# Expert tiles of 256 gathered rows instead of 512 in the mixture-of-experts stage, with three weight buffers

## The chip, the cores and the metric

One NeuronCore of one Trainium2 chip runs the whole program. The metric is the device time of one execution in microseconds (us). The kernel before takes 4466.64 us, the median of three runs (4465.85 to 4473.64).

## The reference

Four layers follow each other on x of shape (4, 1024, 256): L0 to L3, each an attention against a context of 77 tokens and then a block of its own (L0: causal self-attention and a mixture of experts; L1: a ternary MLP; L2: a butterfly MLP; L3: a self-attention with selected heads). The change concerns the mixture of experts of L0:

```
logits = flat @ gate_W + gate_b                    # 4096 tokens x 8 experts
top_v, top_i = top_k(logits, 2); w = softmax(top_v)
for e in range(8):
    mid = gelu(flat @ exp_W1[e] + exp_b1[e])       # 256 -> 1024
    out += w_full[:, e:e+1] * (mid @ exp_W2[e] + exp_b2[e])   # 1024 -> 256
```

Only the two chosen experts of a token have a weight that isn't zero, so 8192 pairs of token and expert are worth computing.

## The kernel before, in words

The program has three phases, parted by barriers. Phase 0 runs the two attentions and the gate of L0 for each of the 4 batches. It writes the normalised tokens to DRAM (`d_xn`), the tokens themselves to `d_s`, and for each pair of token and expert an entry (token, gate weight) to the table `d_tab`, which has a region of 4096 places for each expert. It also splits the expert weights into a high and a low f16 half and stores them in `d_moe`, 2 MB for an expert (two DMAs of 1024 KB). Phase 1 is the expert stage. Phase 2 runs all the rest, batch by batch.

**The expert stage** works on tiles of TILE = 512 gathered rows of one expert. The number of tiles is a constant: NTILE (line 33) is the most that 8192 entries on 8 experts can need, 23 for 512 rows. All are run, whatever the gate chose; tiles without entries work on rows that nobody reads. At its start VectorE works out the expert and the region of each tile (lines 2290 to 2307), one column for each tile. Then each tile i goes through these steps, and every engine has its order written out by hand:

- SyncE (SP), lines 695 to 735: `tile_table(i)` waits until the stores of tile i-4 have landed, reads the tile's numbers into registers and loads 512 table entries (line 703). `tile_weights(i)` waits for the last matmul of tile i-2, loads the 2 MB of weights into `Wm[i % 2]` (line 712), and the bias columns into `b1t[i % 2]` (line 716). SP runs two tiles ahead. In its iteration 2 it also loads the context keys and values for phase 2 (`load_keys`, lines 556 to 559).
- GpSimd (POOL), lines 1719 to 1743: `pick_rows(i)` gathers the rows in TC4 = 4 indirect DMAs of 128 rows (line 1725); `add_rows(i - 2)` follows it and adds the results to `d_s` in 4 indirect DMAs (line 1734), after VectorE has written them and the adds of the tile before have landed.
- TensorE (PE): `turn_rows(i)` transposes the picked rows in 8 transposes (line 1226), in the middle of tile i-1, after `up(i-1, 4)`. `up(i, m)`, m = 0 to 7, computes 128 hidden channels for the 512 rows by `split3` (lines 806 to 808: high by high, high by low, low by high), 6 matmuls of 512 columns. `down(i, m)` adds the part of hidden group m to the output, 12 matmuls of 256 columns, one triple for each 128 rows, with 2 bias matmuls more for each 128 rows at m = 7 (lines 1252, 1253). `down` runs two steps behind `up`.
- ScalarE (ACT): `rows_affine(i)` (line 1594, two instructions) takes the transposed rows with scale and shift; line 1607 is the Gelu of each `up`.
- VectorE (DVE): `rows_parts` and the eight `halves` of a tile split values into f16 halves (lines 1912 and 1914); `rows_out(i - 1)` (line 2321, one instruction for each 128 rows) multiplies the output of the tile before by the gate weights, after `halves` of m = 3.

The order of PE's work:

```
for n in range(len(order) + 2):
    if n < len(order):
        up(*order[n])
        if order[n][1] == 4 and order[n][0] + 1 < NTILE:
            turn_rows(order[n][0] + 1)
    if n >= 2:
        down(*order[n - 2])
```

and POOL's:

```
for i in range(NTILE + 2):
    if i < NTILE:
        pick_rows(i)
    ...
    if i >= 2:
        add_rows(i - 2)
```

Of the kernel before, what the change touches and what calls it, by code (L numbers as in the profile page):

```python
# [7 lines left out]
P = 128  # L8
NB, T, D, TC = 4, 1024, 256, 77
NT = T // P  # L10
KD = D // P
# [192 lines left out]
def build(nc, A, out, known, stages):  # L204
    led = Ledger(known)
    with ExitStack() as ctx:
# [63 lines left out]
        def area(kb, n, dt=F32, rows=P):  # L270
# [35 lines left out]
        before_p, idf, tile_n, row_n = route[:, 0:P], route[:, 128:136], route[:, 136:136 + NTILE], route[:, 160:161]  # L306
# [13 lines left out]
        over = route[:, 816:816 + NTILE * NE].rearrange("p (i e) -> p i e", e=NE)  # L320
        passed = route[:, 1000:1000 + NTILE * NE].rearrange("p (i e) -> p i e", e=NE)
        tile_e, tile_j = route[:, 1184:1184 + NTILE], route[:, 1208:1208 + NTILE]
# [5 lines left out]
        sel = area(62.5, 32, F16)  # L328
# [3 lines left out]
        XTm = XT[:, :, :, :].rearrange("p s k c -> p (s k c)").rearrange("p (n s k c) -> p n s k c", n=2, s=2, k=KD)  # L332
# [74 lines left out]
        d_moe = dram("scr_expert_weights", [NE, 2, P, 2 * KD * HID], F16)  # L407


        names = ["pe", "act", "dve", "pool", "ld_next", "ld_kvw", "ld_const", "ld_kx", "st_kx0", "st_kx1", "st_vx0", "st_vx1", "st_mask", "ld_b12", "st_q0", "st_q1", "st_k0", "st_k1",  # L410
                 "ld_stack0", "ld_stack1", "ld_m0", "ld_m1", "ld_wexp0", "ld_wexp1", "st_wexp0", "st_wexp1",
                 "st_xn", "st_s", "st_tab", "ld_tab0", "ld_tab1", "ld_tab2", "ld_tab3", "ld_b10", "ld_b11", "ld_pick0", "ld_pick1",
                 "st_y", "ld_sel", "st_out"] + [f"{n}{g}" for n in ("ld_s", "ld_r") for g in range(NG)] + [
                 f"{n}{p}{c}" for n in ("st_qc", "ld_qc", "ld_mc") for p in range(2) for c in range(2)]
        sems = {n: ctx.enter_context(nc.semaphore("s_" + n)) for n in names}
# [77 lines left out]
        def _(sp):  # L493

            sp.dma_start(identf[:], A["c_ident"]).then_inc(once["low_w"], 16)
            sp.dma_start(d_tab, A["c_none"]).then_inc(once["kvw"], 16)
            sp.dma_start(route[:, 0:161], A["c_route"]).then_inc(once["kvw"], 16)
# [208 lines left out]
            def tile_weights(i):  # L706

                e = where[i][1]
                if i >= 2:
                    sp.wait_ge(*of("pe", "D", i - 2, NM - 1))  # L710
                for w in range(2):
                    sp.dma_start(Wm[i % 2][:, w].rearrange("p s n -> p (s n)"),
                                 d_moe[bass.ds(e, 1), w].rearrange("o p n -> p (o n)")).then_inc(*did(f"ld_wexp{i % 2}", i, w))
                if i >= 2:
                    sp.wait_ge(*of("act", "free", "U", i - 2, NM - 1))
                sp.dma_start(b1t[i % 2], A["exp_b1"][bass.ds(e, 1)].rearrange("o p m -> p (o m)")).then_inc(*did(f"ld_b1{i % 2}", i))
# [5 lines left out]
            sp.dma_start(b1b, A["L1_b1"].partition_broadcast(P)).then_inc(*did("ld_b12", 0))  # L722
            sp.dma_start(b2b, A["L1_b2"].partition_broadcast(P)).then_inc(*did("ld_b12", 1))
# [58 lines left out]
        def _(pe):  # L782
# [436 lines left out]
            def experts():  # L1219

                def turn_rows(i):
                    s = claim("A", "T", i)
                    pe.wait_ge(*of(f"ld_pick{i % 2}", i, TC4 - 1))
                    for c in range(TC4):
                        for k in range(KD):
                            mm = pe.transpose(s[:, k * TILE + c * P:k * TILE + (c + 1) * P], picked[:, i % 2, c, k * P:(k + 1) * P], identf[:])
                    mm.then_inc(*did("pe", "T", i))

                def up(i, m):
                    if m == 0:  # L1230
                        pe.wait_ge(*of(f"ld_wexp{i % 2}", i, 1))
                        pe.wait_ge(*of("dve", "xlo", i))
                    s = claim("A", "U", i, m)
                    w1 = Wm[i % 2][:, 0].rearrange("p s (k n) -> p s k n", k=KD)
                    for k in range(KD):
                        mm = split3(s[:, 0:TILE], parts(w1, k, slice(m * P, (m + 1) * P)), parts(XTm[:, i % 2], k), k == 0, k == KD - 1)
                    mm.then_inc(*did("pe", "U", i, m))

                def down(i, m):
                    n = i * NM + m  # L1240
                    if m == 0:
                        pair = ("B0", "B1") if i % 2 == 0 else ("S0", "S1")
                        acc[:] = [claim(pair[0], "D", i, 0), claim(pair[1], "D", i, 1)]
                    pe.wait_ge(*of("dve", "midlo", i, m))
                    w2 = Wm[i % 2][:, 1].rearrange("p s (m n) -> p s m n", m=NM)
# [10 lines left out]
                acc = [None, None]  # L1256
# [101 lines left out]
        def _(act):  # L1358
# [228 lines left out]
            def experts():  # L1587
# [11 lines left out]
                for i in range(NTILE):  # L1599
                    for m in range(NM):  # L1600
                        act.wait_ge(*of("pe", "U", i, m))
                        if m == 0:
                            act.wait_ge(*of(f"ld_b1{i % 2}", i))
# [3 lines left out]
                        act.activation(midf[:, n % 3], slot("U", i, m)[:, 0:TILE], ACT.Gelu, bias=b1t[i % 2][:, m:m + 1],  # L1607
                                       scale=1.0 / WS).then_inc(*frees("act", "U", i, m))
                        if m == 4 and i + 1 < NTILE:
                            rows_affine(i + 1)  # L1610
# [841 lines left out]
def layouts(i):  # L2452
# [37 lines left out]
    qs[0] = BIG  # L2490
    ks = z((MROW + 2 - 48, 2, GH, T), np.float16)
    ks[MROW - 48:] = 1.0
    route = z((P, 161), np.float32)
# [3 lines left out]
    route[:, 160] = np.arange(P) - BROW.index("e0")  # L2497
# [52 lines left out]
```

## Time and profile before

| what | value |
|---|---|
| median of three runs | 4466.64 us |
| the profiled execution's own time | 4502.6 us |
| its span | 4500.8 us |
| expert stage, first table step on DVE to the first load of phase 2 | 1641.3 to 2200.9 us of the span |
| PE / DVE / ACT / POOL busy over the whole span | 78% / 51% / 33% / 9% |
| HBM read and written over the span | 167.5 MB, 77.3 MB |

The profile is of one execution. Busy time of PE is a union of overlapping matmuls: successive matmuls start closer together than one of them lasts, so the distance of two starts, and not the duration, is what a matmul costs. A row of the groups has the line, the engine, the operation, out<-in by name, the shapes and the count; behind the bar stand the busy time in us and the mean duration in ns, then the idle time just before and what ended it.

### The profile page before, as it was taken

The page shows a single profiled execution, that of the slowest core. Times are in us where ns is not written, and L with a number is a line of the kernel's source. Part 1 is how long each engine was busy: PE and PEld are TensorE (multiplying, and loading weights), DVE is VectorE, ACT ScalarE, POOL GpSimd, SP SyncE. Part 2 cuts the span into 40 slices and gives each one's busy share as a digit, 9 for nine tenths or more (in the row PEclk, how much of TensorE's full clock was granted, in tenths as well). Part 3 has the DMA queues.
Part 4 walks back from the last instruction along what each step waited for, and adds up shares of the span by engine and source line. Part 5 has one row for each costly group of instructions (what it writes and reads, how often), then busy time and mean ns, then how long its engine had stood idle before and what let it go on. Part 6 is the DMA issues. An engine that isn't in the chain of part 4 may idle for free.

```text
span 4500.8 us, 51861 instructions
## 1 busy us (share of the span) xinstructions
PE 3497.8 (78%) x20322; PEld 1826.0 (41%) x20322; DVE 2298.6 (51%) x4977; ACT 1488.1 (33%) x2106; POOL 390.4 (9%) x298
## 2 busy tenths in 40 slices
PE   5278677667767749999778888788787896878969
PEld 2133332332332336666434433345343452444524
DVE  8765465565465335555463443643436534355343
ACT  2124333433334323333243322443224432234322
POOL 6000001001000124444200000000000000000000
PEclk7668868967877869999889989999899998999989
DMA  3221221231131056555401222012211113011130
GB/s 121 85 56 16 100 57 16 69 88 16 36 121 16 19 121 140 141 141 141 88 10 25 30 54 48 11 25 28 57 32 26 25 25 60 25 34 25 25 60 10
DMA packets 203902, 249.63 MB, mean 55 GB/s; under 512 B 99985, under 2 KB 166179, under 8 KB 191781
## 3 DMA queue, kind: packets, MB, share of 16 engines
q1 hardware_dynamic: 183945, 222.06, 19.3%
q0 software_dynamic: 19712, 24.20, 3.4%
q8 instruction: 167, 2.74, 0.3%
q14 instruction: 78, 0.63, 0.0%
HBM read 167.53 MB, written 77.25 MB: 54 GB/s over the span
## 4 chain that ended last, share of the span: by engine, by line
PE 53%; DVE 25%; ACT 7%; DMA 7%; issue 5%; SPq 2%; POOL 1%; another core or an unknown queue 1%; DVEq 0%; ACTq 0%; POOLq 0%
PE ps L806 5%; PE ps L808 5%; PE ps L807 5%; PE ps L1342 5%; DVE max_parts L1992 4%; PE ps L859 4%; PE ps L991 3%; PE ps L953 3%; PE ps L1199 2%; PE ps L1206 2%; PE ps L974 2%; ACT arena L1512 2%; PE ps L1127 2%; DVE minus_max_context L2136 2%; DMA q_stack<-scr_q 1%
## 5 line engine op out<-in xcount | busy, mean ns | idle before, releaser
L859 PE MATMUL ps<-ternary_W,ident 128*128 128x512 f16 x1552 | 496.2, 410 | 80.5 <-issue 25.4
L1992 DVE TENSOR_REDUCE max_parts<-ps 128x1 f32<-128x512 f32 (+3 forms) x768 | 388.5, 551 | 251.4 <-PE ps L956 151.8
L1444 ACT ACTIVATE arena<-ps 128x256 f32<-128x256 f32 (+7 forms) x512 | 321.4, 650 | 508.3 <-PE ps L974 289.2
L953 PE MATMUL ps<-k_stack,q_stack 96*128 96x512 f16 (+3 forms) x768 | 272.5, 390 | 101.0 <-DVE max_parts L1992 57.6
L1912 DVE CAST arena<-arena 128x512 f16<-128x512 f32 (+2 forms) x296 | 143.0, 483 | 316.1 <-ACT arena L1607 201.0
L974 PE MATMUL ps<-q_stack,k_stack 98*128 98x512 f16 (+3 forms) x768 | 257.6, 382 | 39.8 <-ACT arena L1444 24.4
L1512 ACT ACTIVATE arena<-ps 77x1024 f32<-77x1024 f32 x192 | 190.4, 1016 | 279.3 <-PE ps L1119 274.4
L859 PEld LDWEIGHTS ps<-ternary_W,ident 128*128 128x128 f16 x1552 | 153.4, 104 | 314.8 <-issue 113.7
L2414 DVE TENSOR_REDUCE max_parts<-ps 128x1 f32<-128x512 f32 x256 | 170.1, 688 | 176.1 <-PE ps L1317 174.1
L1342 PE MATMUL ps<-arena 128*96 128x512 f32 x512 | 246.1, 592 | 1.7 <-ACT arena L1671 1.7
L1914 DVE TENSOR_TENSOR arena<-arena 128x512 f16<-128x512 f32 (+2 forms) x296 | 239.0, 808 | 10.2
L1607 ACT ACTIVATE arena<-ps,arena 128x512 f32<-128x512 f32 x184 | 126.4, 687 | 354.9 <-PE ps L808 353.0
L1671 ACT ACTIVATE arena<-ps 128x1024 f32<-128x1024 f32 x128 | 130.5, 1023 | 338.6 <-PE ps L1331 338.6
L953 PEld LDWEIGHTS ps<-k_stack,q_stack 96*128 96x128 f16 x768 | 76.8, 103 | 339.1 <-DVE max_parts L1992 254.8
L806 PE MATMUL ps<-x_channels_hi_lo,arena 128*128 128x512 f16 x432 | 168.3, 389 | 52.4 <-DVE arena L2401 48.7
L808 PE MATMUL ps<-arena 128*128 128x256 f16 (+1 forms) x752 | 204.5, 272 | 0.0
L807 PE MATMUL ps<-arena 128*128 128x256 f16 (+1 forms) x752 | 204.4, 272 | 0.0
L806 PE MATMUL ps<-arena 128*128 128x256 f16 (+1 forms) x752 | 204.1, 272 | 0.0
L2136 DVE TENSOR_REDUCE minus_max_context<-ps 128x4 f32<-128x308 f32 x384 | 157.5, 467 | 86.6 <-PE ps L1103 85.4
L991 PE MATMUL ps<-arena 128*32 128x512 f32 (+3 forms) x1536 | 179.9, 552 | 13.5 <-ACT arena L1444 13.5
L1708 POOL DMA_INDIRECT scr_taken<-v_context,slots_of_batch x64 | 61.8, 966 | 1430.7 <-DVE slots_of_batch L2281 1412.4
L1734 POOL DMA_INDIRECT scr_x<-q_stack,arena x92 | 151.3, 1645 | 257.4 <-DVE q_stack L2321 236.4
(429 smaller groups left out, 7059.8 us busy)
## 6 DMA issues: line engine op xcount, KB each, us to landing
arena<-scr_expert_weights SPq DMA_DIRECT2D x46, 1024.0 KB
q_stack<-in_exp_W SPq DMA_DIRECT2D x16, 1024.0 KB
scr_expert_weights<-k_stack SPq DMA_DIRECT2D x16, 1024.0 KB, 4.9
q_stack<-scr_q SPq DMA_DIRECT2D x120, 128.0 KB, 3.8
scr_q<-arena SPq DMA_DIRECT2D x48, 256.0 KB, 2.9
k_stack<-scr_q SPq DMA_DIRECT2D x72, 128.0 KB, 4.1
scr_q<-arena SPq DMA_DIRECT2D x16, 512.0 KB, 4.3
scr_k<-arena SPq DMA_DIRECT2D x16, 512.0 KB, 4.5
```

The costliest lines, as they stand in the source:

```text
L806: pe.matmul(o, left[0], right[0], start=first, stop=False, **kw)
L807: pe.matmul(o, left[0], right[1], start=False, stop=False, **kw)
L808: return pe.matmul(o, left[1], right[0], start=False, stop=last, **kw)
L859: pe.matmul(s[:, 0:CH], ident[:], Wq1[:, 0, 0:CH], start=True, stop=True)
L953: mm = pe.matmul(s[:, 0:n], QS[0:MROW, buf, j, t * P:(t + 1) * P], KS[0:MROW, buf, j, c * CH:c * CH + n], start=True, stop=not on_edge)
L974: mm = pe.matmul(o, KS[0:MROW + 2, buf, j, kt * P:(kt + 1) * P], QS[0:MROW + 2, buf, j, a:(c + 1) * CH], start=True, stop=not edge)
L991: mm = pe.matmul(acc[c][QUARTER * j:QUARTER * (j + 1), a - c * CH:CH], v, p, start=kt == 0, stop=final, tile_position=(0, QUARTER * j))
L1342: pe.matmul(acc[c][0:TV], VP4[:, kt, h, :], PR4[:, (h * NT + kt) % NP, c * CH:(c + 1) * CH], start=kt == 0, stop=kt == NT - 1).then_inc(*d ...
L1444: act.activation(PR[:, n % NP, kt * P:T], slot(L, "ST", g, kt, j)[:, kt * P:T], ACT.Exp).then_inc(*did("act", L, "exp", g, kt, j))
L1512: act.activation(PRc[c][:, n % 3].rearrange("p i c -> p (i c)"), slot(L, "ST", c, g, jp)[0:TC], ACT.Exp).then_inc(*did("act", L, "exp", c, ...
L1992: dve.tensor_reduce(mpart[:, j * NT + t, c:c + 1], slot(L, "S", g, t, j, c)[:, 0:n], AX, ALU.max).then_inc(*frees("dve", L, "S", g, t, j, c))
L2136: dve.tensor_reduce(mine, slot(L, "S", c, g, t)[:, 0:GH * TC].rearrange("p (j c) -> p j c", c=TC), AX, ALU.max, negate=True).then_inc(*fre ...
```

## The change

TILE goes from 512 to 256, so NTILE goes from 23 to 39 and TC4 from 4 to 2. The three weight buffers `Wm[i % 3]` are the two of before and the space of the key stack `KS`, which phase 1 doesn't use otherwise. SP runs three tiles ahead; the bias columns have four buffers. Output accumulators of a tile are one PSUM bank (B0 or S0 by turns) where they were two. The tables of the start of the stage, which have 39 columns now, lie in the space of `XT`. The core of the diff:

```diff
-TILE = CH
+TILE = 2 * P
...
-        Wm = [area(16 + 16 * i, 2 * 2 * KD * HID, F16).rearrange("p (w s n) -> p w s n", w=2, s=2) for i in range(2)]
-        midf = area(48, 3 * CH).rearrange("p (n c) -> p n c", n=3)
-        mid = area(54, 4 * 2 * CH, F16).rearrange("p (n s c) -> p n s c", n=4, s=2)
+        Wm = [w.rearrange("p (w s n) -> p w s n", w=2, s=2) for w in (area(16, 2 * 2 * KD * HID, F16), area(32, 2 * 2 * KD * HID, F16),
+                                                                      KS[:, :, :, :].rearrange("p b h c -> p (b h c)"))]
+        midf = area(48, 3 * TILE).rearrange("p (n c) -> p n c", n=3)
+        mid = area(54, 4 * 2 * TILE, F16).rearrange("p (n s c) -> p n s c", n=4, s=2)
...
-        b1t = [area(63.25 + 0.0625 * i, NM) for i in range(2)]
+        b1t = [area(63.25 + 0.0625 * i, NM) for i in range(4)]
...
             def tile_weights(i):
                 e = where[i][1]
-                if i >= 2:
-                    sp.wait_ge(*of("pe", "D", i - 2, NM - 1))
+                if i >= 3:
+                    sp.wait_ge(*of("pe", "D", i - 3, NM - 1))
                 for w in range(2):
-                    sp.dma_start(Wm[i % 2][:, w].rearrange("p s n -> p (s n)"),
+                    sp.dma_start(Wm[i % 3][:, w].rearrange("p s n -> p (s n)"),
...
-                if i >= 2:
-                    sp.wait_ge(*of("act", "free", "U", i - 2, NM - 1))
+                if i >= 4:
+                    sp.wait_ge(*of("act", "free", "U", i - 4, NM - 1))
-                sp.dma_start(b1t[i % 2], ...)
+                sp.dma_start(b1t[i % 4], ...)
-            for i in range(2):
+            for i in range(3):
                 tile_table(i)
                 tile_weights(i)
...
             for i in range(NTILE):
-                if i + 2 < NTILE:
-                    tile_table(i + 2)
-                    tile_weights(i + 2)
+                if i + 3 < NTILE:
+                    tile_table(i + 3)
+                    tile_weights(i + 3)
...
-                        pair = ("B0", "B1") if i % 2 == 0 else ("S0", "S1")
-                        acc[:] = [claim(pair[0], "D", i, 0), claim(pair[1], "D", i, 1)]
+                        acc[:] = [claim("S0" if i % 2 else "B0", "D", i, 0)]
```

`tile_table`, `pick_rows`, `add_rows` and the orders of PE, ACT and DVE are the same in their text; their loops over TC4 have two passes instead of four.

## Rows read from the trace of the kernel before

**Rows 1.** The page: busy time, share of the span and instructions of each engine.
```profile
PE 3497.8 (78%) x20322; PEld 1826.0 (41%) x20322; DVE 2298.6 (51%) x4977; ACT 1488.1 (33%) x2106; POOL 390.4 (9%) x298
```

**Rows 2.** Busy time by stretch: us, busy us (count) by engine, granted clock, DMA share, GB/s.
```profile
1660.00:1700.00 40.00, 35.68 (x226) 23.49 (x227) 17.95 (x31) 12.62 (x18) 6.90 (x8) 0.88 0.45 144
1700.00:1800.00 100.00, 97.21 (x692) 67.89 (x691) 53.05 (x96) 31.08 (x45) 47.68 (x35) 1.00 0.67 136
```

**Rows 3.** Timeline of PE in a tile: start us, us, engine, line, operation.
```profile
1850.70 0.38 PE L806 MATMUL ps<-x_channels_hi_lo,arena 128*128 128x512 f16 x1
...
1852.00 0.27 PE L806 MATMUL ps<-arena 128*128 128x256 f16 x1
1852.11 0.27 PE L807 MATMUL ps<-arena 128*128 128x256 f16 x1
```

**Rows 4.** Chain that ended last, 1770 to 2195: start us, us, what (first, last of 17).
```profile
1793.09 0.87 PE ps L1226 x8
...
2154.47 0.87 PE ps L1226 x8
```

**Rows 5.** Groups by line and shape, expert stage.
```profile
L1914 DVE TENSOR_TENSOR arena<-arena 128x512 f16<-128x512 f32 x184 | 127.4, 693 | 6.3
L1607 ACT ACTIVATE arena<-ps,arena 128x512 f32<-128x512 f32 x184 | 126.4, 687 | 354.9 <-PE ps L808 353.0 <-DVE x_channels_hi_lo L1912 1.9
```

**Rows 6.** Groups by line and shape, whole span, ACT: one function at two widths.
```profile
L1444 ACT ACTIVATE arena<-ps 128x512 f32<-128x512 f32 x64 | 37.8, 597 | 74.4 <-PE ps L976 73.3
...
L1444 ACT ACTIVATE arena<-ps 128x256 f32<-128x256 f32 x64 | 23.0, 382 | 36.7 <-PE ps L976 36.6
```

**Rows 7.** Groups by line and shape, whole span, DVE: instructions of 256 columns.
```profile
L2200 DVE TENSOR_TENSOR x_tokens<-x_tokens,weights_flat 128x256 f32<-128x256 f32 x32 | 13.6, 425 | 1.1
...
L2082 DVE TENSOR_SCALAR arena<-arena 128x256 f16<-128x256 f32 x32 | 7.1, 283 | 0.0
```

**Rows 8.** Timeline of POOL: first add and last gather of one round.
```profile
1862.07 1.62 POOL L1734 DMA_INDIRECT scr_x<-q_stack,arena  x1 [9.72 <-DVE q_stack L2321]
...
1873.91 1.03 POOL L1725 DMA_INDIRECT x_tokens<-scr_x_normalised,arena  x1 [0.30 <-issue]
```

**Rows 9.** Busy time by stretch, after that last gather (columns as rows 2).
```profile
1877.00:1878.00 1.00, 1.00 (x6) 0.47 (x5) 0.00 (x0) 0.00 (x0) 0.00 (x0) 1.00 0.00 0
```

**Rows 10.** Chain in the one round beside the key loads: gather to landing.
```profile
1763.20 6.97 DMA x_tokens<-scr_x_normalised,arena
```

**Rows 11.** Timeline of SP's queue: weights, then the next table load.
```profile
1854.52 0.85 SPq L712 DMA_DIRECT2D arena<-scr_expert_weights  x2
...
1857.20 0.39 SPq L703 DMA_DIRECT2D arena<-scr_taken  x1
```

**Rows 12.** Timelines of SP's queue and POOL: table load behind the key loads, its reader.
```profile
1749.83 4.96 SPq L703 DMA_DIRECT2D arena<-scr_taken  x1
...
1759.20 1.01 POOL L1725 DMA_INDIRECT x_tokens<-scr_x_normalised,arena  x1 [5.52 <-DMA arena<-scr_taken]
```

**Rows 13.** DMA queues, 1855 to 1877: packets, MB, share of 16 engines.
```profile
q0 software_dynamic: 768, 1.05, 30.5%
q1 hardware_dynamic: 960, 2.11, 26.5%
```

**Rows 14.** Who waited for whom, 1665 to 2187: us, times, longest us.
```profile
PE ps L1226 <- DMA x_tokens<-scr_x_normalised,arena: 2.8, 1, 2.8
```

**Rows 15.** Timeline at the start of the stage: first transposes, first matmul of tile 0.
```profile
1660.63 1.97 PE L1226 MATMUL ps<-identf,x_tokens 128*128 128x128 f32 x8 [28.04 <-DMA x_tokens<-scr_x_normalised,arena]
...
1666.29 0.59 PE L806 MATMUL ps<-x_channels_hi_lo,arena 128*128 128x512 f16 x1 [3.69 <-DVE x_channels_hi_lo L1914]
```

**Rows 16.** Timeline at the end of the stage: last results on DVE, last add, next load.
```profile
2189.72 1.66 DVE L2321 TENSOR_SCALAR q_stack<-ps,arena 128x256 f32<-128x256 f32 x4 [2.86 <-PE ps L1253]
...
2197.22 1.55 POOL L1734 DMA_INDIRECT scr_x<-q_stack,arena  x1 [0.30 <-issue]
2200.94 0.39 SPq L521 DMA_DIRECT2D h_tokens<-scr_x  x1
```

More of the change, by code:

```diff
@@ L319, in build @@
         n_tiles, up_to = route[:, 800:808], route[:, 808:816]
-        over = route[:, 816:816 + NTILE * NE].rearrange("p (i e) -> p i e", e=NE)
-        passed = route[:, 1000:1000 + NTILE * NE].rearrange("p (i e) -> p i e", e=NE)
-        tile_e, tile_j = route[:, 1184:1184 + NTILE], route[:, 1208:1208 + NTILE]
-        Wm = [area(16 + 16 * i, 2 * 2 * KD * HID, F16).rearrange("p (w s n) -> p w s n", w=2, s=2) for i in range(2)]
-        midf = area(48, 3 * CH).rearrange("p (n c) -> p n c", n=3)
-        mid = area(54, 4 * 2 * CH, F16).rearrange("p (n s c) -> p n s c", n=4, s=2)
+        tables = XT[:, :, :, :].rearrange("p s k c -> p (s k c)").bitcast(F32)
+        over, passed = (tables[:, 320 * i:320 * i + NTILE * NE].rearrange("p (i e) -> p i e", e=NE) for i in range(2))
+        tile_e, tile_j = tables[:, 640:640 + NTILE], tables[:, 704:704 + NTILE]
+        Wm = [w.rearrange("p (w s n) -> p w s n", w=2, s=2) for w in (area(16, 2 * 2 * KD * HID, F16), area(32, 2 * 2 * KD * HID, F16),
+                                                                      KS[:, :, :, :].rearrange("p b h c -> p (b h c)"))]
+        midf = area(48, 3 * TILE).rearrange("p (n c) -> p n c", n=3)
+        mid = area(54, 4 * 2 * TILE, F16).rearrange("p (n s c) -> p n s c", n=4, s=2)
         tile_ids = area(62, 2 * NTILE).bitcast(I32)
-        sel = area(62.5, 32, F16)
+        sel = area(62.5, 64, F16)
         taken = [area(63 + 0.0625 * i, 2 * TC4).rearrange("p (c w) -> p c w", w=2) for i in range(4)]
-        b1t = [area(63.25 + 0.0625 * i, NM) for i in range(2)]
+        b1t = [area(63.25 + 0.0625 * i, NM) for i in range(4)]
         picked = X[:, :, :].rearrange("p (n c) d -> p n c d", n=2)
-        XTm = XT[:, :, :, :].rearrange("p s k c -> p (s k c)").rearrange("p (n s k c) -> p n s k c", n=2, s=2, k=KD)
+        XTm = XT[:, :, :, :].rearrange("p s k c -> p (s k c)")[:, 0:2 * 2 * KD * TILE].rearrange("p (n s k c) -> p n s k c", n=2, s=2, k=KD)
         q_f32 = QS[:, :, :, :].rearrange("p b h c -> p (b h c)").bitcast(F32)
@@ L496, in _ @@
             sp.dma_start(d_tab, A["c_none"]).then_inc(once["kvw"], 16)
-            sp.dma_start(route[:, 0:161], A["c_route"]).then_inc(once["kvw"], 16)
+            sp.dma_start(route[:, 0:200], A["c_route"]).then_inc(once["kvw"], 16)
             sp.dma_start(low_w, A["low_w"]).then_inc(once["low_w"], 16)
@@ L708, in tile_weights @@
                 e = where[i][1]
-                if i >= 2:
-                    sp.wait_ge(*of("pe", "D", i - 2, NM - 1))
+                if i >= 3:
+                    sp.wait_ge(*of("pe", "D", i - 3, NM - 1))
                 for w in range(2):
-                    sp.dma_start(Wm[i % 2][:, w].rearrange("p s n -> p (s n)"),
-                                 d_moe[bass.ds(e, 1), w].rearrange("o p n -> p (o n)")).then_inc(*did(f"ld_wexp{i % 2}", i, w))
-                if i >= 2:
-                    sp.wait_ge(*of("act", "free", "U", i - 2, NM - 1))
-                sp.dma_start(b1t[i % 2], A["exp_b1"][bass.ds(e, 1)].rearrange("o p m -> p (o m)")).then_inc(*did(f"ld_b1{i % 2}", i))
-            for i in range(2):
+                    sp.dma_start(Wm[i % 3][:, w].rearrange("p s n -> p (s n)"),
+                                 d_moe[bass.ds(e, 1), w].rearrange("o p n -> p (o n)")).then_inc(*did(f"ld_wexp{i % 3}", i, w))
+                if i >= 4:
+                    sp.wait_ge(*of("act", "free", "U", i - 4, NM - 1))
+                sp.dma_start(b1t[i % 4], A["exp_b1"][bass.ds(e, 1)].rearrange("o p m -> p (o m)")).then_inc(*did(f"ld_b1{i % 4}", i))
+            for i in range(3):
                 tile_table(i)
@@ L721, in _ @@
             sp.dma_start(KX[:MROW + 2], A["c_kx"]).then_inc(*did("ld_const", 0))
-            sp.dma_start(b1b, A["L1_b1"].partition_broadcast(P)).then_inc(*did("ld_b12", 0))
-            sp.dma_start(b2b, A["L1_b2"].partition_broadcast(P)).then_inc(*did("ld_b12", 1))
+            sp.dma_start(b1b, A["L1_b1"].partition_broadcast(P)).then_inc(*did("ld_rows12", 0))
+            sp.dma_start(b2b, A["L1_b2"].partition_broadcast(P)).then_inc(*did("ld_rows12", 1))
             for i in range(NTILE):
-                if i + 2 < NTILE:
-                    tile_table(i + 2)
-                    tile_weights(i + 2)
+                if i + 3 < NTILE:
+                    tile_table(i + 3)
+                    tile_weights(i + 3)
                 if i == 2:
@@ L1230, in up @@
                     if m == 0:
[L1231 removed]
+                        pe.wait_ge(*of(f"ld_wexp{i % 3}", i, 1))
                         pe.wait_ge(*of("dve", "xlo", i))
                     s = claim("A", "U", i, m)
[L1234 removed]
+                    w1 = Wm[i % 3][:, 0].rearrange("p s (k n) -> p s k n", k=KD)
                     for k in range(KD):
@@ L1254, in down @@
                     mm.then_inc(*did("pe", "D", i, m))
-                acc = [None, None]
+                acc = [None]
                 turn_rows(0)
@@ L1602, in experts @@
                         if m == 0:
-                            act.wait_ge(*of(f"ld_b1{i % 2}", i))
+                            act.wait_ge(*of(f"ld_b1{i % 4}", i))
                         n = i * NM + m
@@ L1606, in experts @@
                             act.wait_ge(*of("dve", "midlo", *back(i, m, 3)))
-                        act.activation(midf[:, n % 3], slot("U", i, m)[:, 0:TILE], ACT.Gelu, bias=b1t[i % 2][:, m:m + 1],
+                        act.activation(midf[:, n % 3], slot("U", i, m)[:, 0:TILE], ACT.Gelu, bias=b1t[i % 4][:, m:m + 1],
                                        scale=1.0 / WS).then_inc(*frees("act", "U", i, m))
@@ L2492, in layouts @@
     ks[MROW - 48:] = 1.0
-    route = z((P, 161), np.float32)
+    route = z((P, 200), np.float32)
     route[:, :P] = k_ < q_
@@ L2496, in layouts @@
     route[:, 136:136 + NTILE] = np.arange(NTILE)
-    route[:, 160] = np.arange(P) - BROW.index("e0")
+    route[:, 199] = np.arange(P) - BROW.index("e0")
     none = z((ROWS, 2), np.float32)
```

10 lines of the change are left out of this document (5 added, 5 removed).

## The prediction

> **What bounds the kernel now.** I read the page first: PE is busy for 78% of the span, more than any other engine [rows 1]. Then the expert stage by stretches: from 1700 to 1800 PE is busy for 97.2 of 100 us at a granted clock of 1.00, DVE for 53, ACT for 31, POOL for 48, and the DMA engines are 67% busy [rows 2]. So the stage is PE's work and hardly anything else. The chain that ended last agrees: the transposes of successive tiles stand on it at a distance of (2154.47 - 1793.09) / 16 = 22.586 us, without a wait between them [rows 4]. In the whole stretch of full tiles PE waits once, 2.8 us for a gather [rows 14]. A tile lasts as long as its matmuls, so fewer columns are less time as long as nothing else comes late.
>
> What a matmul costs is the distance of two starts [rows 3]. Six matmuls of 512 columns (one `up`) take 1852.00 - 1850.70 = 1.30 us, 0.217 each. Those of 256 columns (`down`) start 0.109 us apart. A tile is 8 x 1.30 = 10.4 for `up`, 8 x 12 x 0.109 = 10.46 for `down`, 8 x 0.109 = 0.87 for the bias rows and 0.87 for the eight transposes [rows 4], together 22.6, which is the period.
>
> **The change part by part.**
>
> PE's work. A tile of 256 rows has 48 `up` matmuls and 48 `down` matmuls, all of 256 columns, 4 bias matmuls and 4 transposes: 100 x 0.109 + 0.435 = 11.34 us. 39 of these are 442.1 us, where 23 x 22.586 = 519.5 us stand now. The removed part is rows that belong to no token: 39 x 256 = 9984 rows are computed instead of 23 x 512 = 11776. This is **-77.4 us**, all of it on the path. That the 256-column `up` costs 0.109 isn't shown as such; `down` has the same shape at this price, also with a new weight load for each matmul. Half of 0.217 is the lower end, and the unchanged 0.217 the upper (a rival below).
>
> ACT and DVE. A step of PE (`up` and `down`) shrinks from 2.6 to 12 x 0.109 = 1.31 us, so their fixed costs count more. Gelu takes 0.687 for 512 columns [rows 5]; a Copy falls from 0.597 to 0.382 when its width is halved [rows 6], so I take 0.687 - 0.215 = 0.47. DVE's two parts of a step take 0.283 and 0.425 at 256 columns [rows 7] (the second is 0.693 at 512 [rows 5]), 0.71 together. With `rows_out` (2 x 0.41 [rows 16]) and `rows_parts` (about 1.0) DVE has 8 x 0.71 + 0.83 + 1.0 = 7.5 us of work in 11.34, and ACT about 5. From the end of an `up` to the ready halves it is 0.47 + 0.71 + 0.2 of gaps = 1.4 us; PE asks for them four half steps of 0.65 later, 2.6 us. Even behind `rows_out` (0.83) this fits. Cost: nothing; the cover is 1.2 us, 0.4 in that one step.
>
> POOL. Its instructions shrink in number with the rows: 2 adds of 1.62 and 2 gathers of about 1.0, each with 0.30 before it [rows 8], 6.5 us in 11.34. What counts is when the last gather lands. I take the end of `up(j, 3)` as zero. Halves until 1.4, `rows_out` until 2.2, POOL's first add at 2.5 (an estimated 0.3 us after DVE's end, like POOL's gaps [rows 8]), then two adds of 1.92 and a gather of 1.3 with their gaps: the gathers of tile j+2 are issued at 6.3 and 7.6. Their rows are needed by the transposes after `up(j+1, 4)`, at 11.34 + 1.31 = 12.65. That leaves **5.0 us** from the issue of the last gather. Now such a gather is issued at 1873.91 and by 1877.00 no byte moves [rows 8, 9]: 3.1 us at most, so 1.9 us to spare. The one gather that met weights and key loads on the DMA engines took 6.97 us [rows 10], 2.0 too many.
>
> DMA. The weights of a tile stay 2 MB, but come every 11.34 us. Now they take 26.5% of 22 us = 5.8 us of all 16 engines, gathers and adds 30.5% = 6.7 us for 512 rows [rows 13]. After it is 5.8 + 3.35 = 9.2 of 11.34, 81% busy. So the transfers fit, but no longer stand apart. On the scale above, SP can issue the weights of tile j+2 when `down(j-1, 7)` is done, at -1.9, three half steps ahead of zero. They hold the engines until about 5.7 to 7.5 with the adds between them, and the gathers come at 6.3 to 8.6, just behind. With three buffers the weights have until the start of tile j+2, some 18 us, for a transfer of 7. The table load of tile j+2 now goes out ahead of these weights where it followed them 2.7 us later [rows 11], so it lands earlier within the tile. I take the uncontended 3.1 us, since the order of issue keeps the gathers behind most of the weights. Cost zero; the other end is 2.0 us for each tile.
>
> The key loads. They hold up SP's queue once, so that a table load takes 4.96 us to issue and its gather starts 9.4 us after it [rows 12]; PE's 2.8 us are its result [rows 14]. In a tile half as long this hurts more; between 0 and 7 us, I take 4.8, **+2.0 us**.
>
> Start and end of the stage. The first matmul of tile 0 comes 5.66 us after the first transpose [rows 15]. Two gathers fewer (2 x 1.33 [rows 8]), four transposes fewer (1.0 of 1.97 [rows 15]) and about a third of the other 3.7 us for ACT and DVE make 5.0. Against it stand wider tables (312 elements instead of 184, an estimated 0.5) and 2 MB more of weights beside the first gathers (1.0, estimated; 0 to 5). **-3.5 us**. At the end the last results take 1.66 us and four adds follow, the last from 2197.22 to its landing at 2200.94 [rows 16]; two results and two adds fewer, 0.8 + 2 x 1.85: **-4.5 us**.
>
> PE's clock falls at a start: 0.88 from 1660 to 1700 [rows 2], as before and once. Loads of constants for the tables change by a few hundred KB at most, in phase 0, hidden behind its work: nothing.
>
> **The sum** is -77.4 + 2.0 - 3.5 - 4.5 = -83.4 us. The profiled execution took 4502.6 us and would take 4419.2. It lies 36 us above the median, so the difference, not the time, is carried over: 4466.6 - 83.4 = **4383.2 us**.
>
> **The rivals.**
>
> *Late gathers.* If the gathers of each tile meet the weights, they need 6.97 instead of 3.1 us [rows 10] and the period becomes 7.6 + 7.0 - 1.31 = 13.3 us. That is 2.0 us for each of 38 tiles: 4383 + 74 = 4457 us. For it: 81% DMA use, and the adds now fall into the weights' time, which delays SP's next table and weights. Against it: only 2 gathers queue up, and the weights have a lead of 6 us. Partial lateness lies between.
>
> *Slow table loads, slower than before.* If in each tile the table load lands 9.4 us after its issue, as the one behind the keys did [rows 12], it is there at 7.9 (issued near -1.5, when the adds of tile j-2 have landed). The gathers then start at 7.9 and 9.2 and land at 16.2: 3.5 us late, 38 times, 4383 + 133 = 4516 us. This decides from 83.4 / 38 = 2.2 us of lateness for each tile. Against it: the load had waited behind four strided key loads, which stand there once.
>
> *The change doesn't halve `up`.* If a weight load for each 256 columns held `up` at 0.217, 39 x 48 x 0.108 = 202 us are added: 4585 us. `down`, with as many weight loads for a column, speaks against it.
>
> *A cold clock.* If PE ran at 1.2 GHz in each tile because it waits in each, every matmul costs twice: 39 x 22.7 = 885 us, 366 more than now, 4832 us. Against it: the wait of 2.8 us lies within 1700 to 1800, and the granted clock there is 1.00 [rows 2, 14]. The Trainium skill (TensorE: Matmul & The Clock Gate, section HAM oscillation) speaks for this rival: where the matmuls of a tile are shorter than a wait for DMA, the clock is throttled in each tile, and the advice is to pad rows to 512 or more. By this rule the change goes the wrong way; the trace doesn't bear it out, since there is no wait for it to start from.
>
> **How the numbers follow.** The forecast has 0.78, late gathers 0.12, slow tables 0.05, `up` not halved 0.03, the cold clock 0.02. The forecast's own range: start at its best (-1.5) and no key stall at all (-4.8) give 4377, half of the 8 us between the runs makes 4373; upwards 5 for the keys and 3.5 for the start give 4392. The stated range goes from 4372 to 4425, which takes in gathers that come late by up to 1.1 us a tile. A measurement of this kernel can tell about 0.2%, 9 us, from no change. Faster by more is the forecast and most of the late gathers, 0.87; within 0.2% 0.03; slower 0.10.
>
> **What would show it.** The stage's transposes should follow each other at 11.3 us, PE be over 97% busy at clock 1.00, DMA near 80%. `up` steps should take 0.65 us. The first load of phase 2 should come some 83 us earlier. Wrong would be: PE's transposes waiting for a gather in each tile (late gathers), POOL waiting for a table load (slow tables), `down` waiting for DVE's halves, or a granted clock under 1.00 between 1700 and the end of the stage.

## The result and the profile after

The changed kernel takes 4400.29 us, the median of four runs (4397.03 to 4408.35), against 4466.25 us for the kernel before: 66.0 us less, ratio 0.9854 with a 95% interval of 0.9834 to 0.9875. The forecast was 83.4 us less and 4383.2 us; the measured time lies within its range, 17 us above the predicted value.

The profiled execution has a span of 4406.7 us, 94 us under that of before. Only 65.4 us of them are of the expert stage; the rest lies in phases that the change doesn't touch. What lies outside the stage differs by more than that among all the kernels profiled here (3889 to 3955 us), though it is the same work in each, and by 12 us between three profiles of the changed kernel. So the stage is read by itself: from the first table step on DVE to the first load of phase 2. It took 559.7 us (1641.27 to 2200.94) and takes 494.3 us now. The timeline of the changed kernel at both ends of the stage, columns as in [rows 15]:

```profile
1608.48 0.17 DVE L2290 TENSOR_SCALAR v_context<-v_context 128x8 f32<-128x8 f32 x1 [5.24 <-SPq L535]
...
1628.51 0.37 PE L807 MATMUL ps<-x_channels_hi_lo,arena 128*128 128x256 f16 x1 [2.46 <-DVE x_channels_hi_lo L1914]
...
2095.56 0.88 DVE L2321 TENSOR_SCALAR q_stack<-ps,arena 128x256 f32<-128x256 f32 x2 [1.36 <-DMA scr_x<-q_stack,arena]
...
2098.97 1.55 POOL L1734 DMA_INDIRECT scr_x<-q_stack,arena  x1 [0.30 <-issue]
...
2102.79 0.39 SPq L522 DMA_DIRECT2D h_tokens<-scr_x  x1
```

From the first table step to the first matmul of tile 0 it is 20.0 us (25.0 before), from there to the last matmul 467.0 us (523.4), and from the last matmul (2095.5) to the load 7.3 us (11.3). What is missing from the gain is in the middle. The stretches there, to be set beside [rows 2]:

```profile
1700.00:1800.00 100.00, 96.10 (x874) 85.34 (x872) 63.77 (x169) 40.03 (x84) 47.91 (x35) 1.00 0.72 223
1800.00:1900.00 100.00, 96.46 (x877) 85.72 (x876) 63.44 (x170) 40.32 (x85) 45.19 (x33) 1.00 0.72 220
```

PE has gaps where it had next to none: 3.5 to 4 us in 100. The granted clock stays at 1.00 in these stretches all the same. The waits of the stage say for what, beside [rows 14]:

```profile
PEld ps L1227 <- ACT arena L1607: 14.2, 13, 1.7
PE ps L1227 <- DMA x_tokens<-scr_x_normalised,arena: 13.7, 17, 2.4
...
POOL x_tokens L1725 <- DMA arena<-scr_taken: 0.9, 1, 0.9
```

PE waits 17 times for a gather before the transposes, 2.4 us at most. The wait put down to ACT is taken for the same wait, since e9 below removes both rows together: the Gelu named there only frees the PSUM slot. POOL hardly ever waits for a table. So it is the gathers' own landing, and the chain that ended last has it on it:

```profile
1821.56 5.51 DMA x_tokens<-scr_x_normalised,arena
...
1827.20 0.63 PE ps L1227 x4
...
1832.76 6.77 DMA x_tokens<-scr_x_normalised,arena
...
1839.66 0.63 PE ps L1227 x4
```

These two gathers take 5.51 and 6.77 us to land, where the forecast had counted on 3.1 at most and found 5.0 bearable. The issues between 1710 and 2050 with the median time to landing (the last number):

```profile
arena<-scr_expert_weights SPq DMA_DIRECT2D x38, 1024.0 KB, 7.6
...
scr_x<-q_stack,arena POOLq DMA_INDIRECT x58, 8.4
x_tokens<-scr_x_normalised,arena POOLq DMA_INDIRECT x58, 5.6
...
arena<-scr_taken SPq DMA_DIRECT2D x28, 2.0 KB, 1.8
```

The adds need 8.4 us; the last one of the kernel before, with nothing beside it, took 2200.94 - 2197.22 = 3.7 [rows 16]. Adds, gathers and weights run beside each other. When do the weights go out?

```profile
1656.05 0.85 SPq L713 DMA_DIRECT2D arena<-scr_expert_weights  x2
...
1658.16 0.60 PE L1227 MATMUL ps<-identf,x_tokens 128*128 128x128 f32 x4
...
1720.21 0.63 PE L1227 MATMUL ps<-identf,x_tokens 128*128 128x128 f32 x4 [0.86 <-DMA x_tokens<-scr_x_normalised,arena]
...
1721.34 0.85 SPq L713 DMA_DIRECT2D arena<-scr_expert_weights  x2
```

At 1656.05 they go out 2.1 us ahead of a tile's transposes, or 9.2 us after those of the tile before (1646.81). At 1721.34 they go out 1.1 us after the transposes, some 3 us later in the tile. In the 30 tiles from there on this place is between 0.4 and 1.6 us after the transposes. What SP waits for meanwhile is the landing of the adds, where in the kernel before it was PE's last matmul alone (us, times, longest; before from 1665 to 2190, changed from 1665 to 2100):

```profile
SPq L712 <- PE ps L1253: 409.8, 21, 36.4
```

```profile
SPq L701 <- DMA scr_x<-q_stack,arena: 281.0, 34, 9.3
```

The distances of the transposes are 10.52 us at first, then 11.35 until the key loads, then 13.90 and 13.05, then between 11.35 and 12.98, 11.90 on the average of all 38.

The two long distances at the key loads have two causes. Only the first has a late gather. Behind it the clock falls:

```profile
1680.00:1690.00 10.00, 7.61 (x55) 5.96 (x53) 4.74 (x12) 3.00 (x7) 5.02 (x4) 0.83 0.93 155
```

```profile
1683.42 0.63 PE L1227 MATMUL ps<-identf,x_tokens 128*128 128x128 f32 x4 [2.39 <-DMA x_tokens<-scr_x_normalised,arena]
...
1684.70 0.42 PE L808 MATMUL ps<-x_channels_hi_lo,arena 128*128 128x256 f16 x1
1684.91 0.42 PE L809 MATMUL ps<-x_channels_hi_lo,arena 128*128 128x256 f16 x1
```

PE waits 2.39 us, and from 1684.5 to 1688.0 its matmuls of 256 columns start 0.21 us apart instead of 0.109: it runs at the lower of the clock's two levels (1.2 and 2.4 GHz). That is the 13.05 - 11.35 = 1.7 us of the second distance, in which the profile shows no wait of PE. In the kernel before, a wait of 2.8 us at the same place had no such sequel: its matmuls of 512 columns still start 0.22 us apart right behind it.

The instructions themselves came out as worked out from [rows 5 to 7]. Groups by line and shape in the changed kernel:

```profile
L1607 ACT ACTIVATE arena<-ps,arena 128x256 f32<-128x256 f32 x312 | 148.0, 474 | 259.4 <-PE ps L809 246.8 <-DVE arena L1912 10.0 <-DVE x_channels_hi_lo L1914 2.5
L1914 DVE TENSOR_TENSOR arena<-arena 128x256 f16<-128x256 f32 x312 | 133.4, 427 | 10.8
...
L1912 DVE CAST arena<-arena 128x256 f16<-128x256 f32 x312 | 96.2, 308 | 160.4 <-ACT arena L1607 153.0 <-PE ps L809 5.1
```

### The profile page after: what moved, and what is told of

Same layout as the page of the kernel before. It is cut to its first block, busy times and chain, and to the rows that moved or that the text cites. A ratio compares the mean times of both kernels' runs of the same rounds, so it can differ in the third digit from the quotient of the medians.

```text
span 4406.7 us, 53693 instructions
## 1 busy us (share of the span) xinstructions
PE 3436.6 (78%) x20698; PEld 1862.0 (42%) x20698; DVE 2314.3 (53%) x5251; ACT 1516.7 (34%) x2266; POOL 360.3 (8%) x270
## 4 chain that ended last, share of the span: by engine, by line
PE 51%; DVE 26%; DMA 9%; ACT 7%; issue 4%; SPq 2%; POOL 1%; DVEq 0%; ACTq 0%; another core or an unknown queue 0%
PE ps L1342 5%; PE ps L807 4%; DVE max_parts L1992 4%; PE ps L808 4%; PE ps L809 4%; PE ps L860 4%; PE ps L992 4%; PE ps L954 3%; PE ps L1200 3%; PE ps L1207 3%; PE ps L975 2%; DMA x_tokens<-scr_x_normalised,arena 2%; ACT arena L1512 2%; DVE minus_max_context L2136 2%; PE ps L1128 2%
## 5 line engine op out<-in xcount | busy, mean ns | idle before, releaser
L1912 DVE CAST arena<-arena 128x256 f16<-128x256 f32 (+3 forms) x424 | 161.0, 380 | 239.2 <-ACT arena L1607 153.0
L1914 DVE TENSOR_TENSOR arena<-arena 128x256 f16<-128x256 f32 (+3 forms) x424 | 245.0, 578 | 14.6
L1607 ACT ACTIVATE arena<-ps,arena 128x256 f32<-128x256 f32 x312 | 148.0, 474 | 259.4 <-PE ps L809 246.8
L807 PE MATMUL ps<-x_channels_hi_lo,arena 128*128 128x256 f16 (+1 forms) x480 | 142.7, 297 | 51.1 <-DVE arena L2401 48.7
L2151 DVE RECIPROCAL inverse_sums_by_token<-ps 128x32 f32<-128x32 f32 x48 | 17.2, 358 | 264.2 <-PE ps L1138 264.2
L1734 POOL DMA_INDIRECT scr_x<-q_stack,arena x78 | 133.9, 1716 | 234.2 <-DVE arena L1912 121.7
L975 PEld LDWEIGHTS ps<-q_stack,k_stack 98*128 98x128 f16 x768 | 81.1, 108 | 163.0 <-ACT arena L1444 84.1
L808 PE MATMUL ps<-x_channels_hi_lo,arena 128*128 128x256 f16 (+1 forms) x480 | 142.8, 297 | 0.0
```

The lines of the kernel that those rows point to most:

```text
L807: pe.matmul(o, left[0], right[0], start=first, stop=False, **kw)
L808: pe.matmul(o, left[0], right[1], start=False, stop=False, **kw)
L975: mm = pe.matmul(o, KS[0:MROW + 2, buf, j, kt * P:(kt + 1) * P], QS[0:MROW + 2, buf, j, a:(c + 1) * CH], start=True, stop=not edge)
L1914: dve.tensor_tensor(lo, src, hi, ALU.subtract).then_inc(*step(*key))
```

## The experiments

**Theory A**: the landing of the adds holds SP up before its table load (`tile_table` waits for the stores of tile i-4), the weights behind it in SP's order go out late, and these share the DMA engines with the next adds and gathers. **Theory B**: the volume on the DMA engines alone makes gathers late, in whatever order things are issued. All experiments start from the changed kernel unless told otherwise, and are read by the distance of the transposes and the length of the stage in one profile each; the whole time differs by 6 to 38 us between executions of one kernel, as much as these effects or more.

**e1: eight table buffers.**

```diff
-                if i >= 4:
-                    sp.wait_ge(*of("st_y", i - 4, TC4 - 1))
+                if i >= 8:
+                    sp.wait_ge(*of("st_y", i - 8, TC4 - 1))
...
-                sp.dma_start(taken[i % 4], ...)
+                sp.dma_start(taken[i % 8], ...)
```

> Eight table buffers instead of four, so that SP's table load of tile i waits for the stores of tile i-8, not i-4. Theory A (the landing of the adds holds up SP, SP issues the weights late, and these meet the next gathers): the weights are issued right after the last matmul of tile i-3, gathers land in 3 to 4 us, the mean distance of the transposes falls from 11.90 to about 11.4 us, and the stage gets about 16 us shorter (4384). Theory B (the volume on the DMA engines alone makes gathers late, whatever the order of issue): the distance stays between 11.8 and 12.0 us and the time near 4400.

Stage 477.4 us, 16.9 less than the changed kernel. Two distances at the key loads are 14.0 and 13.2, one after them is 11.38, all others from the second on 11.35. The weights go out 8.4 us after the transposes (once 8.7) in every tile but the two at the key loads. Ratio 0.9792 (0.9760 to 0.9824); this chip ran the kernel before at 4502 us, so its 4410.5 us are not to be set beside 4400.3. Theory B is out: the same bytes in the same number of DMAs, and away from the keys no gather is late.

**e2: two weight buffers, two tiles ahead** (`Wm[i % 2]`, wait for the last matmul of tile i-2).

> Tiles of 256 rows with two weight buffers, loaded two tiles ahead, all else as in the changed kernel. If the third buffer carries part of the gain: weights issued when the last matmul of tile i-2 is done have some 8.6 us until the next tile but one begins and need 8 to 9 us beside gathers and adds, so PE waits for weights in each tile, 0.5 to 3 us each: a distance of 12 to 14.5 us, 4410 to 4500 us. If the third buffer is idle capital: 11.9 us and 4400 us.

Stage 514.1 us, 19.8 more than the changed kernel; distances between 11.35 and 15.54, and one of 23.3 at the key loads. Of these, (23.3 + 13.4) - (13.9 + 13.05) = 9.7 us fall at the key loads. Ratio 0.9871 (0.9843 to 0.9899), beside 0.9792 for e1 on the same chip; by the whole time alone it can't be told from the changed kernel's 0.9854. PE does wait for weights now, which it never does with three buffers:

```profile
PEld ps L807 <- DMA arena<-scr_expert_weights: 16.1, 13, 4.5
...
PE ps L807 <- DMA arena<-scr_expert_weights: 12.5, 10, 4.3
```

The third buffer carries part of the gain, at the lower end of what was expected. The granted clock is 0.95 from 1700 to 1800, where the key loads are, and 0.97 in the next 100 us.

**e3: half the bytes.** Of the weights only the high halves are loaded from tile 3 on.

```diff
-                    sp.dma_start(Wm[i % 3][:, w].rearrange("p s n -> p (s n)"), ...)
+                    n = 2 * KD * HID if i < 3 else KD * HID
+                    sp.dma_start(Wm[i % 3][:, w].rearrange("p s n -> p (s n)")[:, 0:n], ...)
```

> From tile 3 on only the high halves of the expert weights are loaded (1 MB instead of 2 MB for each tile; the low halves are left from the first tiles, so the outputs of the stage are not the reference's). Theory A and B both expect the DMA engines at 45 to 50% in the stage, gathers that land in about 3.5 us and a distance of 11.35 to 11.4 us. If gathers were late because of POOL's or the queue's own latency and not because of the weights, the distance would stay at 11.9 us.

Stage 477.6 us, every distance 11.35 apart from the first (10.34) and the two at the keys (14.96, 13.00); DMA 59% busy from 1720 to 2050, more than expected, since gathers and adds alone are 28.6%. The table still waits for the adds, and the weights go out 8.7 to 10.4 us after the transposes. So this order does no harm as long as the transfer is short: it takes a late start of the weights and their length together.

**e4: gathers a tile earlier.** Eight table buffers, four buffers `picked[:, i % 4]`, and in POOL's loop `add_rows(i - 3)` behind `pick_rows(i)`.

> Eight table buffers and four buffers for gathered rows; POOL gathers tile i before it adds tile i-3 (was i-2), so each gather has one tile more to land. Theories A and B: even a gather of 7 us is in time, PE waits for none, 11.35 us a tile apart from the tiles at the key loads, about 17 us less than the changed kernel (4383). If something else than the gathers holds the transposes (the PSUM slot behind the Gelu, as some of the waits are put down to ACT), the distance stays above 11.6 us.

Stage 479.2 us, distances 11.35 but for the first and two at the keys (15.70, 13.86). Nothing more is won than with e1, so nothing but the gathers had held the transposes up: not the PSUM slot either. Ratio 0.9810 (0.9783 to 0.9837).

**e5 and e11: the changed kernel again**, beside the next ones.

> The changed kernel itself once more, as the base for the runs beside it on this chip. Both theories: ratio to the kernel before 0.985 (0.983 to 0.988), transposes 11.9 us apart, stage 494 us.

> The changed kernel beside the two others on the same chip: stage 494 us, transposes 11.9 us apart, ratio 0.983 to 0.987.

Stages of 494.1 and 491.7 us, ratios 0.9830 (0.9803 to 0.9858) and 0.9853 (0.9830 to 0.9877). The effect is the kernel's and not the execution's; the two distances at the key loads were 16.07 and 13.91, 16.28 and 13.61 here, so 7.3 and 7.2 us over two regular tiles, and 4.3 in the first profile. The second distance is again that of the lower clock: PE waits once, 4.5 and 4.8 us, and behind that its matmuls start 0.21 us apart for a while, which costs 2.6 and 2.3 us.

**e6: eight table buffers, keys in SP's last iteration** (`if i == NTILE - 1` instead of `if i == 2` before the key loads).

> Eight table buffers, and SP loads the context keys after the last weights (iteration 38) instead of in iteration 2. Theory A: no tile at the keys is late any more, all transposes 11.35 us apart, the stage 477.4 - 4.5 = 473 us, 21 us less than the changed kernel, ratio near 0.980. If the two late tiles at the key loads had another cause (start of the weights' queue, ordering of the first tables), they stay at 14.0 and 13.2 us and the stage at 477 us.

The two late tiles are gone (the others are 11.35 but for the first, 9.85, and one of 11.55), but the last distance is 15.5 us: with nothing more to load, SP reaches its last iteration while the last gathers are still to come, and the keys meet them. Stage 477.4 us, no gain over e1. Ratio 0.9831 (0.9808 to 0.9854), not to be told from the changed kernel beside it (0.9830).

**e7: the kernel before with three weight buffers**, tiles of 512 rows.

> The kernel before with the three weight buffers loaded three tiles ahead and nothing else: tiles of 512 rows. PE is busy without a gap at 22.59 us a tile, so a third buffer has nothing to give: stage 557 to 562 us, within 3 us of the kernel before. A rival: 2 MB more at the start delay the first gathers and cost up to 5 us.

Stage 556.7 us, ratio 1.0001 (0.9981 to 1.0020). All distances are 22.59 but the first; the 25.5 at the key loads is gone, and that is the 3 us. By itself the third buffer is worth nothing that the whole time shows.

**e8: tiles of 128 rows** (71), with eight table buffers.

> Tiles of 128 rows (71 of them, 9088 rows), eight table buffers and three weight buffers. Rows alone would give 71 x 5.7 = 403 us, 39 us less than 39 tiles of 256. Two limits speak against: 2 MB of weights take 5.8 us of all DMA engines and gather and add of 128 rows 1.7 more, 7.5 us a tile; and 48 matmuls of 128 columns need a weight load of about 0.10 us each, so that PE needs 24 x 0.109 + 48 x 0.10 = 7.5 us. Either gives 7.5 to 8.5 us a tile, a stage of 555 to 630 us, slower than the kernel before or level with it. Whether PE waits for DMA or PEld is busy throughout tells the two apart.

Stage 590.4 us, 7.95 us a tile, and the first of the two limits is the nearer one. A stretch and the hardware queue's share from 1800 to 2100:

```profile
1900.00:2000.00 100.00, 84.51 (x982) 72.50 (x983) 64.92 (x246) 46.77 (x130) 34.42 (x26) 0.95 0.91 307
```

```profile
q1 hardware_dynamic: 22308, 81.65, 74.7%
q0 software_dynamic: 7319, 9.99, 15.8%
```

The DMA engines are 91% busy and PE 85%. Between 1700 and 2200 PE waits 45 times for a gather, 70.2 us in all and 3.2 at most, and the granted clock is 0.95 to 0.97, so a part of the 7.95 us is the clock's. PE's own work is less than I said, since a matmul of 128 columns with its weight load costs 0.055 us and not 0.10 (the groups by line, with the weight loads' 102 ns, then the timeline):

```profile
L807 PEld LDWEIGHTS ps<-x_channels_hi_lo,k_stack 128*128 128x128 f16 x272 | 27.7, 102 | 11.5 <-issue 6.8 <-ACT q_stack L1594 2.5 <-ACT arena L1607 0.4
```

```profile
1901.18 0.22 PE L807 MATMUL ps<-x_channels_hi_lo,k_stack 128*128 128x128 f16 x1
1901.23 0.22 PE L808 MATMUL ps<-x_channels_hi_lo,k_stack 128*128 128x128 f16 x1
1901.29 0.22 PE L809 MATMUL ps<-x_channels_hi_lo,k_stack 128*128 128x128 f16 x1
```

**e9: eight table buffers, keys behind the last gather.**

```diff
-                if i == 2:
+                if i == NTILE - 1:
+                    sp.wait_ge(*of(f"ld_pick{i % 2}", i, TC4 - 1))
```

> Eight table buffers, and SP loads the context keys only once the gather of the last tile has landed. Theory A (a late tile is one whose gather shares the DMA engines with another load): all 38 distances are 11.35 us but the first, the stage takes 472 us (477.4 less the 4.1 us before the last transposes and 1.4 after them), 22 us less than the changed kernel. If the wait before the last tile in the run before came from the end of the tile loop itself, it stays at 15.5 us. Time of the whole: 0.4 to 0.5% under the changed kernel beside it.

Stage 471.2 us, all distances 11.35 but the first. Median 4382.6 us against 4403.8 for the changed kernel on the same chip (e11), ratio 0.9807 (0.9787 to 0.9828) beside 0.9853 (0.9830 to 0.9877): the two intervals just don't meet, so this version is faster than the changed kernel in its whole time too. Its issues with their landing, and a stretch:

```profile
arena<-scr_expert_weights SPq DMA_DIRECT2D x40, 1024.0 KB, 6.9
...
x_tokens<-scr_x_normalised,arena POOLq DMA_INDIRECT x60, 2.8
...
arena<-scr_taken SPq DMA_DIRECT2D x29, 2.0 KB, 5.2
```

```profile
1800.00:1900.00 100.00, 100.00 (x919) 90.04 (x917) 66.37 (x177) 41.52 (x88) 45.83 (x36) 1.00 0.77 232
```

The gathers land in 2.8 us again, half of the 5.6, with more bytes moved in a second than before, and PE has no gap. The table loads are the ones that travel behind the weights now, 5.2 us instead of 1.8, where that costs nothing.

**e10: only the weights wait for the adds.** Eight table buffers, and ahead of the weights' DMAs:

```diff
+                if i >= 4:
+                    sp.wait_ge(*of("st_y", i - 4, TC4 - 1))
```

> Eight table buffers as before, so the table loads are free, but the weights of tile i wait for the stores of tile i-4, as they do in the changed kernel through SP's order. Theory A: the late issue of the weights is what makes the gathers late, so the distance is back at 11.8 to 12.0 us and the stage at 490 to 496 us. A rival (the late table itself held up POOL): the distance stays at 11.35 us and the stage at 477 us.

Stage 478.8 us, distances 11.35 to 11.48 but for the two at the keys (15.37, 14.03): Theory A fails in this form. The weights go out at 8.4 to 8.8 us in nearly all tiles, so an add that lands in its ordinary time isn't yet in their way. The figures are those of the rival named before the run, a late table that held up POOL. But in the changed kernel POOL waited for a table once, for 0.9 us, so that rival has nothing to stand on.

**e12: only the keys moved**, four table buffers as in the changed kernel. After e10 I had formed **Theory C**: the late order is a second steady state that the key loads set off.

> The changed kernel with four table buffers as it is, and only the context keys moved behind the last gather. Theory C, formed after the wait of the weights for the adds cost nothing: there are two steady orders. In the first, the weights are issued 9.2 us after the transposes, and the adds land early; in the second, entered when the key loads hold SP up, the weights go out 1.2 us after the transposes, the adds need 8.4 us beside them, and so SP's table and weights are late again in every later tile. Without the key loads the second is never entered: all distances 11.35 us, the weights 9.1 to 9.3 us after the transposes throughout, the stage 471 to 474 us. Theory A (the wait for the adds of tile i-4 makes the weights late by itself, keys or not): the tiles drift to 11.8 to 12.0 us after the first few, stage 485 to 490 us.

Theory C falls as well. Stage 485.1 us, with the drift that Theory A expects. SP's weight issues in e12:

```profile
1638.29 0.86 SPq L713 DMA_DIRECT2D arena<-scr_expert_weights  x2
...
1650.42 0.85 SPq L713 DMA_DIRECT2D arena<-scr_expert_weights  x2
...
1661.92 1.74 SPq L713 DMA_DIRECT2D k_stack<-scr_expert_weights  x2
...
1674.51 0.86 SPq L713 DMA_DIRECT2D arena<-scr_expert_weights  x2
```

They follow each other at 12.1, 11.5 and 12.6 us while the tiles still come every 11.35: the last three of these go out 9.2, 9.3 and 10.6 us after the transposes, the next 11.1, and from the second after that some 12.4. No key load is in sight there; the order reinforces itself. The adds land later from tile to tile as well: those issued from 1642.5, 1653.9, 1665.2, 1676.6, 1687.9 and 1699.3 need 4.0, 4.7, 5.6, 6.3, 7.0 and 7.9 us (medians of two). Ratio 0.9826 (0.9800 to 0.9852).

**What the runs together say.** Two causes, nearly independent, by the length of the stage:

| | keys in iteration 2 | keys after the last gather |
|---|---|---|
| four table buffers | 494.3, 494.1, 491.7 us | 485.1 us |
| eight table buffers | 477.4 us | 471.2 us |

The drift costs 14 to 17 us, the keys 6 to 9, of which the lower clock behind the wait is 1.7 to 2.6. Each cell is one profile but the first. The drift needs three things, each of which was taken away alone: the table's wait for the adds (e1), the full length of the weights' transfer (e3), and SP's work between that wait and the weights (e10). In e10 the wait stands directly before the weights. In the changed kernel two register loads and the table's issue lie between; in the kernel before such a piece took from 1855.88 to 1857.59, 1.7 us. With that lead the weights of the first tiles are issued at 9.2 us and not at 8.4, where the last matmul of tile i-3 would allow. Their tail then lies beside the next adds for longer, these land later, and the next weights go out later still, until adds need 8.4 us. That the 1.7 us tip the balance is inferred from e10 and from the 9.2; a kernel with only them removed was not run.

## Why the prediction was right, and where it was off

Direction, the main mechanism (fewer rows) and the range held. One term that was put at nothing was not nothing, and one was too small. The range took this in because it had been drawn up to gathers that come 1.1 us late in each tile. By its steps:

- *PE's work, -77.4 us.* Right. With both disturbances gone (e9) the first to the last matmul of the stage take 444.5 us against 523.4 before, 78.9 less, of which 2.8 are the wait of before [rows 14]. The period is 11.35 us where 11.34 was worked out, and a matmul of 256 columns in `up` costs 0.109 as in `down`. The rival of an `up` that isn't halved is out, and so is a clock that is cold in each tile: the granted clock is 1.00 from 1700 to 2000, although 23 of the 36 distances away from the keys are over 11.4 us. But once, behind the wait of 2.39 us at the key loads, it did fall, for 1.7 us of lost time; the prediction had this for every tile or for none. Of the rule of the Trainium skill (TensorE: Matmul & The Clock Gate, section HAM oscillation), a throttled clock behind a wait for DMA, the trace shows this one case and not its return in each tile; the advice there to pad rows to 512 or more would have given up the gain.
- *ACT and DVE, nothing.* Right: Gelu 0.474 us (0.47 worked out), DVE's two parts 0.308 and 0.427 (0.283 and 0.425), and PE waits for neither.
- *POOL and DMA, nothing.* This is the term that failed: "I take the uncontended 3.1 us, since the order of issue keeps the gathers behind most of the weights. Cost zero". The limit of 5.0 us was right, the landing was not: 5.6 us at the median, so that the tiles away from the keys cost 17.3 us over the regular period in the first profile, 0.5 us a tile. The place of the weights was worked out from the last matmul of tile j-1 alone; SP's wait for the adds in `tile_table`, which stands ahead of the weights in SP's order, was passed over there. The rival of slow tables does reckon with it ("issued near -1.5, when the adds of tile j-2 have landed"), and a table at -1.5 can't be followed by weights at -1.9. That the table load "goes out ahead of these weights" was taken as a gain, where it is what ties the weights to the adds; nor was it new, since in the kernel before, too, a tile's table goes ahead of its own weights (those at 1877.10, after the table at 1857.20 of [rows 11]). The rival of late gathers had the mechanism in its own words (the adds "delay SP's next table and weights") and a price of 74 us for the worst case; a quarter of that came. Slow tables did not happen: 1.8 us to land.
- *The key loads, +2.0 us* on 2.8 before, 4.8 in all. Measured 4.3, 7.3 and 7.2 us in three profiles, and 6 to 9 by the table above. 1.7 to 2.6 us of each are the lower clock, for which the sum had no term.
- *Start -3.5 us*: -5.0. *End -4.5 us*: -4.0.

The sum of the measured parts is (20.0 - 25.0) + (467.0 - 523.4) + (7.3 - 11.3) = -65.4 us, and the medians differ by 66.0. That the two agree so closely is luck: the interval of the ratio allows 56 to 74 us.

## What to carry to other kernels

When tiles get smaller, the engines' work shrinks with them, but the time to landing of a DMA of the same size need not (a gather of 128 rows took 2.8 us with tiles of 512 rows in e7 and of 256 in e9). So each wait for a landing has to be laid out anew on the scale of the new tile, and every queue that issues in order has to be walked from the landing it waits for to the last thing it issues behind it. A wait that only frees a small buffer (here four tables of 2 KB) should not stand ahead of a large load in a queue that issues in order: doubling the number of these buffers was worth 14 to 17 us, about a quarter at most of what the whole change brought. And bulk loads of a later phase belong behind the last latency-bound transfer of this one, not merely behind the last loop iteration (e6 against e9).

## What was not expected of the hardware

- A wait can cost more than its length: behind one of 2.39 us the matmuls of the changed kernel started 0.21 us apart instead of 0.109 for 3.5 us. Behind one of 2.8 us in the kernel before they did not.
- Beside 2 MB of weights a gather of 128 rows takes 5.6 us to land instead of 2.8, and an add of 128 rows 8.4 instead of 3.7, though the DMA engines are busy for 72% of the time, less than in e9 (77%), where they are not late. When the transfers run counts for more than how many there are.
- A matmul of 128 columns with a weight load of its own starts 0.055 us after the one before it (e8), although a weight load is listed with 0.10 us. It is 0.217 at 512 columns, 0.109 at 256 and 0.055 at 128, so at this width, too, columns and not weight loads set the price.
- The whole time of one and the same kernel varies by 6 to 38 us between executions, and the stage hardly: three profiles of the changed kernel agree within 2.6 us. Of the effects within the changed kernel only the largest, e9's 0.5%, is clear in the whole time as well.
